# Edge counts of a graph kernel in groups of 16 destinations instead of 32

## The chip, the cores and the metric

The kernel runs on one core of one Trainium2 chip. The metric is the device time of one execution in microseconds (us); shown are the median of three runs and one profiled execution. Engines: TensorE (PE: matmuls; PEld: its weight loads), VectorE (DVE), ScalarE (ACT), GpSimd (POOL), SyncE (SP, which issues DMAs). Each engine has an instruction queue of its own, which also runs register loads, register arithmetic and branches; in the views these carry a q (DVEq). Engines meet through semaphores: an instruction counts one up when it is done, another waits until the count is high enough.

## The reference

1250 nodes with 768 features each, 40000 directed edges (src, dst) sorted by dst, and two graph blocks one after the other, each with a residual and a layer norm:

```python
def reference(x, src, dst, ...):
    # block 1: layer norm, two attention convolutions (4 heads of 192, then 2 of 96), an output product
    x = _layernorm(x + _L0_gnn_ref(x, edge_index, ...), axis=-1)
    # block 2: two normalized graph convolutions
    x = _layernorm(x + _L1_gnn_ref(x, ...), axis=-1)
    return x

def gat_conv(x, src, dst, W, a_src, a_dst, bias, H, C, n):
    h = (x @ W).reshape(n, H, C)
    e = leaky_relu(s_src[src] + s_dst[dst])
    ee = exp(e - emax[dst])                       # emax: the greatest e of each destination
    alpha = ee / denom[dst]                       # denom: their sum
    out = segment_sum(alpha[:, :, None] * h[src], dst, num_segments=n)
```

In both blocks every node also has an edge to itself. All that the edges contribute can be written with one matrix of counts, ct[source, destination] = how many edges lead from source to destination: the sums over edges become dense products with it.

## The kernel before, in words

Nodes are padded to NP = 1280 and cut into T = 10 tiles of P = 128. Edges lie in 313 chunks of 128; a unit is UC = 2 chunks, 256 edges. The kernel is written for each engine by hand; the order on each engine is the order of the code.

Setup (until about 40 us): weights are loaded and combined, the edge indices are transposed so that an edge's source and destination lie along partitions (sloT: source within its tile; keyT: source tile x 1280 + destination), and for each group of W destinations (a window; group and window mean the same below), VectorE works out which units can hold its edges, since dst is sorted. Four numbers a window go to the row rngrow: the running number of its first extra unit, the one after its last, its first unit, and the count.

Edge counts (from 41 to 204 us, the stage of the change). There are NW = 40 windows of W = 32 destinations, four (WPT) in each tile of destinations. A window takes UW = 4 fixed units from its first unit on, and then as many extra units as its edges need, in a loop whose bounds are loaded from rngrow. For each unit VectorE makes two one-hot matrices (one_hots, L512 and L513): the source one-hot ohs, 128 places x 2 chunks = 256 elements, by comparing iota with sloT, and the destination one-hot ohd, T x W = 320 columns x 2 chunks = 640 elements, which has a one in the column (source tile, destination) and is made by comparing a table vkey with key. TensorE multiplies the two for each chunk (edge_window) and sums all in one PSUM bank: 128 sources x 320 columns. Then one matmul with the identity adds the edges from a node to itself, and ScalarE copies the bank to ctmp (128 x 320). Two banks take turns.

The fixed units go through a ring of RING = 4 places; VectorE waits for a place with unit_used, TensorE for a unit with unit_ready. Extra units have two places of their own (xohs, xohd; extra_used, extra_ready). VectorE's window loads the next window's bounds from rngrow behind its first unit and its second (window_range, L306), TensorE's loads one number behind its second.

Between windows TensorE does other work of the tile: six transposes at its start, twelve dense matmuls (x times the first weights, 388 columns, three behind each window; in the last tile six behind each of the first two), and behind the first window the ten transposes of the tile before, whose counts ScalarE turns into the mask and the degrees. In the last tile VectorE makes the score vector svec before its last window, for which it waits for the last dense result. After the counts come the maxima, the attention heads, and the second block.

TensorE's matmuls of float32 are two records each in the trace.

Of the kernel before, what the change touches and what calls it, by code (L numbers as in the profile page):

```python
# [5 lines left out]
F32, BF16 = mybir.dt.float32, mybir.dt.bfloat16  # L6
# [4 lines left out]
P = 128  # L11
N, E, D = 1250, 40000, 768
T = -(-N // P)
NP = T * P
NR = N - (T - 1) * P
KD = D // P
# [6 lines left out]
W = 32  # L23
NW = NP // W
WPT = P // W
WC = T * W
# [10 lines left out]
UW = 4  # L37
# [24 lines left out]
def build(nc, t_in, out):  # L62
    ctx = ExitStack()
    with ctx:
# [34 lines left out]
        tri = at("tri", [NW, NW], F32, R_MASK + 17408)  # L99
# [31 lines left out]
        ohd_c = at("ohd_c", [P, PR, WC, 2], BF16, R_BIG + 46080)  # L131
        ohs_d = at("ohs_d", [P, PR, P, 2], BF16, R_BIG + 48640)
# [27 lines left out]
        ohs_abc = at("ohs_abc", [P, 3, PR, P, 2], BF16, R_T1)  # L160
        xohs = at("xohs", [P, 2, PR, P, 2], BF16, R_T1 + 3072)
        ohd_ab = at("ohd_ab", [P, 2, PR, WC, 2], BF16, R_T1 + 5120)
        xohd = at("xohd", [P, 2, PR, WC, 2], BF16, R_T1 + 10240)
        ohd_d = at("ohd_d", [P, PR, WC, 2], BF16, R_MASK + (T - 1) * NP * 2)
        vkey1 = at("vkey1", [P, WC, 2], I16, R_T1 + 7680)
        vkey2 = at("vkey2", [P, WC, 2], I16, R_T1 + 8960)
        vkey3 = at("vkey3", [P, WC, 2], I16, R_T1 + 1536)
# [21 lines left out]
        vkey = small("vkey", [P, WC, 2], I16)  # L189
# [120 lines left out]
        def ring_src(slot):  # L310

            return ohs_abc[:, slot, :, :, :] if slot < 3 else ohs_d[:, :, :, :]

        def ring_dst(slot):
            return ohd_ab[:, slot, :, :, :] if slot < 2 else ohd_c[:, :, :, :] if slot == 2 else ohd_d[:, :, :, :]

# [88 lines left out]
        def _(pool):  # L405
# [19 lines left out]
            step(pool.iota(vkey[:, :, :], pattern=[[NP, T], [1, W], [0, 2]], base=0, channel_multiplier=0, **io))  # L425
# [4 lines left out]
            for w, table in enumerate((vkey1, vkey2, vkey3)):  # L430
                pool.iota(table[:, :, :], pattern=[[NP, T], [1, W], [0, 2]], base=W * (w + 1), channel_multiplier=0, **io).then_inc(vkeys_set, 1)
# [11 lines left out]
        def _(v):  # L443
# [71 lines left out]
            def window(q, r, w, limits):  # L515
# [3 lines left out]
                vk, kv = (vkey, vkey1, vkey2, vkey3)[w], key[:, r, :, :]  # L519
                nxt = [end]  # L520
                for j in range(UW):
# [4 lines left out]
                    one_hots(p0, ring_src(slot), ring_dst(slot), vk, kv, unit_ready)  # L526
# [16 lines left out]
            def tile(q, r, behind, last, limits):  # L543

                v.wait_ge(v_own, V0 + q + 1)
                for w in range(3):
                    limits = window(q, r, w, limits)
# [8 lines left out]
                return window(q, r, 3, limits)  # L556
# [282 lines left out]
        def _(a):  # L839
# [54 lines left out]
            def counts_done(q, r):  # L894
                a.wait_ge(win_out, WPT * q + WPT + 2)
                copy(ct[:, :, bass.ds(q * P, P)], ctmp[:, r, :, :], ct_out)
# [10 lines left out]
            def tile(q, r, behind, last):  # L907
# [8 lines left out]
                for w in range(WPT):  # L916
                    if w == WPT - 1 and not last:
                        fixed_place(q + 1, 1 - r)
# [195 lines left out]
        def _(t):  # L1114
# [61 lines left out]
            def edge_window(q, w, limits):  # L1176
                win = WPT * q + w
                first, end = limits
                nxt = [end]
                bank = ps[:, w % 2, 0:WC]  # L1180
                t.wait_ge(win_out, win + 1)
                for j in range(UW):
                    slot = (UW * w + j) % RING
                    t.wait_ge(unit_ready, UW * win + j + 1)
                    for c in range(UC):
                        last = mm(bank, ring_src(slot)[:, c // 2, :, c % 2], ring_dst(slot)[:, c // 2, :, c % 2], j == 0 and c == 0, False, skip_group_check=True)
# [3 lines left out]
                with t.Fori(first, end) as n:  # L1190
                    place = t.snap(n % 2)
                    t.wait_ge(extra_ready, n + 1)
                    for c in range(UC):
                        last = mm(bank, xohs[:, bass.ds(place, 1), c // 2, :, c % 2], xohd[:, bass.ds(place, 1), c // 2, :, c % 2], False, c == UC - 1, skip_group_check=True)
# [369 lines left out]
```

## Time and profile before

| | us |
|---|---|
| median of three runs | 834.28 (833.35 to 835.22) |
| profiled execution | 830.65 |
| its span (first to last instruction) | 828.9 |
| granted clock of TensorE over the span | 0.977 |
| TensorE busy | 787.5 (95%) |
| VectorE busy | 588.5 (71%) |
| ScalarE busy | 296.1 (36%) |

### The profile page before, as it was taken

What the parts mean: (1) busy time and instruction counts of PE and PEld (TensorE: products, weight loads), DVE (VectorE), ACT (ScalarE), POOL (GpSimd) and SP (SyncE); (2) the same over time, 40 slices, a digit from 0 to 9 for tenths busy, and PEclk for the clock granted to TensorE, in tenths of its full rate; (3) what the DMA queues carried; (4) which work ended last, traced back from release to release, by engine and by line L of the source; (5) the groups of instructions that cost most, each with busy time, mean ns of one, the idle gap of its engine ahead of it and who ended that gap; (6) DMA issues with size and microseconds to landing.
All of it is one profiled execution on the core that took longest, in us unless ns stands there. A gap on an engine that the chain in (4) does not pass through costs nothing.

```text
span 828.9 us, 11930 instructions
## 1 busy us (share of the span) xinstructions
PE 787.5 (95%) x4286; PEld 664.6 (80%) x4286; DVE 588.5 (71%) x1210; ACT 296.1 (36%) x577; POOL 24.9 (3%) x36
## 2 busy tenths in 40 slices
PE   5899999998997999999897999899999999999997
PEld 4856666665664999999765899688898889999997
DVE  2788887885999999999698998866635532113444
ACT  4446666664532434334133454222211311111000
POOL 5100000000000400000000000000000000000000
PEclk9999999999989899999999989999999999999999
DMA  9400000000001402010000510000012000000111
GB/s 315 144 2 1 1 2 1 1 2 1 1 1 21 172 1 65 23 42 1 1 0 2 178 29 2 1 1 1 1 39 96 1 1 1 1 1 20 58 58 52
DMA packets 10540, 27.77 MB, mean 33 GB/s; under 512 B 665, under 2 KB 4075, under 8 KB 9968
## 3 DMA queue, kind: packets, MB, share of 16 engines
q1 hardware_dynamic: 10480, 26.97, 9.8%
q8 instruction: 37, 0.61, 0.3%
q14 instruction: 23, 0.19, 0.1%
HBM read 23.09 MB, written 3.88 MB: 33 GB/s over the span
## 4 chain that ended last, share of the span: by engine, by line
PE 80%; DVE 10%; issue 7%; ACT 2%; DMA 1%; SPq 1%; DVEq 0%
PE ps L1116 76%; DVE att L626 2%; DVE att L662 2%; PE ps L1205 1%; DMA edges<-in_dst 1%; PE ps L1410 1%; DVE out L649 1%; PE ps L1226 1%; PE ps L1259 1%; DVE gw1lo L706 1%; DVE scrap1b L508 0%; DVE h2x L649 0%; DVE mx L508 0%; DVE scrap L508 0%; ACT att L969 0%
## 5 line engine op out<-in xcount | busy, mean ns | idle before, releaser
L1116 PE MATMUL ps<-g,att 128*128 128x193 f32 x800 | 133.9, 331 | 6.0 <-DVE att L626 6.0
L1116 PEld LDWEIGHTS ps<-g,att 128*128 128x128 f32 x800 | 133.2, 193 | 6.8 <-issue 6.6
L969 ACT ACTIVATE att<-att,ssrc 128x1250 f32<-128x1250 f32 x60 | 80.2, 1338 | 93.2 <-DVE att L662 93.0
L626 DVE SCALAR_TENSOR_TENSOR att<-att,ct 128x1250 f32<-128x1250 f32 x60 | 88.0, 1467 | 5.0 <-ACT att L969 4.8
L662 DVE SCALAR_TENSOR_TENSOR att<-uB,s 128x1250 f32<-128x1250 f32 x60 | 91.1, 1522 | 0.0
L1116 PE MATMUL ps<-wp,xT 128*128 128x388 f32 x240 | 87.9, 504 | 0.8 <-ACT xT L913 0.8
L1116 PE MATMUL ps<-yhi,ctr 128*128 128x384 f32 x200 | 67.7, 338 | 0.0
L1116 PEld LDWEIGHTS ps<-wp,xT 128*128 128x128 f32 x240 | 42.8, 191 | 25.0 <-issue 1.3
L723 DVE SCALAR_TENSOR_TENSOR ylo_a<-ps,dinv,yhi 128x384 fp32r<-128x384 f32 x32 | 18.9, 614 | 57.5 <-ACT yhi L841 57.4
L1116 PE MATMUL ps<-h2x,att 128*128 128x97 f32 x400 | 51.0, 293 | 4.2 <-DVE att L626 2.8
L1116 PEld LDWEIGHTS ps<-h2x,att 128*128 128x128 f32 x400 | 50.3, 209 | 5.4 <-DVE att L626 4.6
L1116 PE MATMUL ps<-ylo_a,ctr 128*128 128x384 f32 x160 | 54.1, 338 | 0.0
L512 DVE TENSOR_TENSOR ohs_abc<-iota,sloT 128x256 bf16<-128x256 bf16 x120 | 34.7, 289 | 26.5 <-PE ps L1116 25.3
L841 ACT ACTIVATE yhi<-ps,dinv 128x384 fp32r<-128x384 f32 x40 | 22.0, 578 | 86.8 <-PE ps L1116 86.8
L1116 PE MATMUL ps<-ctr,yhi 128*128 128x512 f32 x180 | 44.8, 357 | 0.3 <-issue 0.3
L1116 PE MATMUL ps<-wux,xT 128*128 128x384 f32 x120 | 41.7, 504 | 0.0
L1116 PE MATMUL ps<-gw2lo,yhi 128*128 128x384 f32 x120 | 40.6, 338 | 0.0
L1116 PE MATMUL ps<-wux,xTd 128*128 128x384 f32 x120 | 40.6, 497 | 0.0
L1116 PE MATMUL ps<-gw2hi,yhi 128*128 128x384 f32 x120 | 40.4, 337 | 0.0
L513 DVE TENSOR_TENSOR ohd_ab<-vkey,key 128x640 bf16<-128x640 int16 x80 | 38.7, 483 | 0.2 <-issue 0.2
L1116 PEld LDWEIGHTS ps<-yhi,ctr 128*128 128x128 f32 x200 | 37.5, 188 | 0.0
L1116 PEld LDWEIGHTS ps<-wux,xT 128*128 128x128 f32 x120 | 23.6, 201 | 15.2 <-issue 1.7
(255 smaller groups left out, 1446.2 us busy)
## 6 DMA issues: line engine op xcount, KB each, us to landing
uB<-u_dram SPq DMA_DIRECT2D x4, 1280.0 KB, 5.9
wux<-in_L_gnn_Wu SPq DMA_DIRECT2D x2, 2304.0 KB, 15.7
gw<-in_L_gnn_W SPq DMA_DIRECT2D x2, 2304.0 KB, 10.8
xs<-in_x SPq DMA_DIRECT2D x1, 3456.0 KB
out<-ybuf SPq DMA_DIRECT2D x9, 384.0 KB, 2.3
w<-in_L_gnn_W SPq DMA_DIRECT2D x2, 1152.0 KB, 6.9
w2x<-in_L_gnn_W SPq DMA_DIRECT2D x1, 576.0 KB, 7.4
wuo<-in_L_gnn_Wu SPq DMA_DIRECT2D x1, 576.0 KB
```

The costliest lines, as they stand in the source:

```text
L512: v.tensor_tensor(src_hot, iota[:, None, :, :].to_broadcast([P, PR, P, 2]), sloT[:, bass.ds(p0, PR), None, :].to_broadcast([P, PR, P, 2]), ...
L513: v.tensor_tensor(dst_hot, vk[:, None, :, :].to_broadcast([P, PR, WC, 2]), kv[:, bass.ds(p0, PR), None, :].to_broadcast([P, PR, WC, 2]), A ...
L626: v.scalar_tensor_tensor(a, a, HUGE, ct[:, q, 0:N], ALU.min, ALU.mult).then_inc(att_ready, 1)
L649: last = v.scalar_tensor_tensor(o, src, rden[:, q:q + 1], add, ALU.mult, ALU.add)
L662: v.scalar_tensor_tensor(att[:, n % NA, 0:N], uB[:, hp % 2, 1, 0:N], s08[:, h, q:q + 1], uB[:, hp % 2, 0, 0:N], ALU.add, ALU.max).then_inc ...
L706: v.tensor_tensor(gw1lo[:, c, :], gw1[:, c, :], gw1hi(c, 0, D).bitcast(F32), ALU.subtract).then_inc(gw1_lo, 1)
L723: v.scalar_tensor_tensor(ylo(q, k * HALF, (k + 1) * HALF), ps[:, bank, 0:HALF], scale[:, q:q + 1], y(q, k * HALF, (k + 1) * HALF), ALU.mul ...
L841: a.activation(dst, src, ACT.Copy, **kw).then_inc(done, 1)
L969: a.activation(at_, at_, ACT.Exp, bias=ssrc[:, h, q:q + 1]).then_inc(att_exp, 1)
L1116: return t.matmul(o, lhsT, rhs, start=start, stop=stop, **kw)
L1205: last = t.transpose(ps[:, 4 + k, c * P - c0:(c + 1) * P - c0], ctmp[:, r, c, :], identf[:, :])
L1226: step = t.transpose(ps[:, 4 + k, c * P:(c + 1) * P], xh[:, r, kk * P:(kk + 1) * P], identf[:, :])
```

## The change

A window is now 16 destinations (W = 16): NW = 80 windows, WPT = 8 in a tile. Two windows in turn (WH = 2) fill the two halves of one PSUM bank, so that ScalarE copies as before a bank of 32 destinations, four (WPG) a tile, and the own-edge matmul is made once for both. Each window has UW = 2 fixed units; the ring still has four places. The destination one-hot of a unit has T x 16 = 160 columns, 320 elements. The eight comparison tables stand in one tensor vkeys, made by GpSimd in setup. All bounds, loads and loops that belonged to a window still do, and so there are twice as many of them.

```diff
-W = 32
+W = 16
+WH = 2
 NW = NP // W
 WPT = P // W
+WPG = WPT // WH
+WB = WH * W
...
-UW = 4
+UW = 2
...
-        vkey1 = at("vkey1", [P, WC, 2], I16, R_T1 + 7680)
...
+        ohs = at("ohs", [P, RING, PR, P, 2], BF16, R_T1)
+        ohd = at("ohd", [P, RING, PR, WC, 2], BF16, R_T1 + 3072)
+        vkeys = at("vkeys", [P, WPT, WC, 2], I16, R_T1 + 6912)
...
 # VectorE
                 for j in range(UW):
                     slot = (UW * w + j) % RING
                     v.wait_ge(unit_used, UW * win + j + 1)
                     p0 = nc.s_assert_within(v.snap((unit0 + j) * PR), 0, (UN - 1) * PR,
                                             skip_runtime_bounds_check_because="the first unit was clamped")
-                    one_hots(p0, ring_src(slot), ring_dst(slot), vk, kv, unit_ready)
+                    one_hots(p0, ohs[:, slot, :, :, :], ohd[:, slot, :, :, :], vk, kv, unit_ready)
                     if win + 1 < NW and j < 2:
                         nxt += window_range(v, win + 1, j + 1)
...
-                for w in range(3):
-                    limits = window(q, r, w, limits)
+                for w in range(WPG - 1):
+                    for half in range(WH):
+                        limits = window(q, r, WH * w + half, limits)
...
-                return window(q, r, 3, limits)
+                for half in range(WH):
+                    limits = window(q, r, WPT - WH + half, limits)
+                return limits
...
 # ScalarE
-                    a.wait_ge(win_ps, WPT * q + w + 1 + 2)
+                    a.wait_ge(win_ps, WPG * q + w + 1 + 2)
...
-                    copy(ctmp[:, r, :, w * W:(w + 1) * W], ps[:, w % 2, 0:WC].rearrange("p (a b) -> p a b", b=W), win_out)
+                    copy(ctmp[:, r, :, w * WB:(w + 1) * WB].rearrange("p a (h b) -> p a h b", b=W),
+                         ps[:, w % 2, 0:WH * WC].rearrange("p (h a b) -> p a h b", h=WH, b=W), win_out)
...
 # TensorE
-                bank = ps[:, w % 2, 0:WC]
-                t.wait_ge(win_out, win + 1)
+                bank = ps[:, group % 2, half * WC:(half + 1) * WC]
+                if half == 0:
+                    t.wait_ge(win_out, WPG * q + group + 1)
...
-                mm(ps[:, w % 2, bass.ds(q * W, W)], identb[:, :], identb[:, w * W:(w + 1) * W], False, True, skip_group_check=True).then_inc(win_ps, 1)
+                if half == WH - 1:
+                    own = ps[:, group % 2, 0:WH * WC].rearrange("p (h n) -> p h n", h=WH)[:, :, q * W:(q + 1) * W]
+                    mm(own, identb[:, :], identb[:, group * WB:(group + 1) * WB].rearrange("p (h b) -> p h b", b=W), False, True, skip_group_check=True).then_inc(win_ps, 1)
...
-                    if not last or w < 2:
-                        k = w if last else w // 2
-                        cs = range(KD) if last else range(3 * (w % 2), 3 * (w % 2) + 3)
+                    if not last or w < 2 * WH:
+                        k = w // WH if last else w // WPG
+                        cs = range(3 * (w % 2), 3 * (w % 2) + 3) if last else range((3 * (w % WPG) + 1) // 2, (3 * (w % WPG) + 4) // 2)
...
-                    if w == 0 and behind:
+                    if w == WH - 1 and behind:
```

How the change moves instructions on VectorE: a stretch of a window in the first tile before, from the load behind the second unit to the loop over the extra units (TENSOR_LOAD reads a register from rngrow; ISA and REGISTER_ALU are register arithmetic, with the wait where one is named).

```order
L306 TENSOR_LOAD rngrow
L512 ISA [waits unit_used]
L512 TENSOR_TENSOR ohs_abc<-iota,sloT 128x256
L513 REGISTER_ALU
L513 TENSOR_TENSOR ohd_c<-vkey_122,key 128x640
L512 ISA [waits unit_used]
L512 TENSOR_TENSOR ohs_d<-iota,sloT 128x256
L513 REGISTER_ALU
L513 TENSOR_TENSOR ohd_d<-vkey_122,key 128x640
L529 UNCONDITIONAL_BRANCH
L529 ISA
L512 ISA [waits extra_used]
```

And the same of the second window now, from the load behind its first unit on:

```order
L303 TENSOR_LOAD rngrow
L502 ISA [waits unit_used]
L502 TENSOR_TENSOR ohs<-iota,sloT 128x256
L503 REGISTER_ALU
L503 TENSOR_TENSOR ohd<-vkeys,key 128x320
L303 TENSOR_LOAD rngrow
L519 UNCONDITIONAL_BRANCH
L519 ISA
L502 ISA [waits extra_used]
L502 ISA
L502 TENSOR_TENSOR xohs<-iota,sloT 128x256
L503 ISA
```

Two units without a load stood between the second load and the loop; now the loop follows at once.

On TensorE, before, where the last matmuls of one window meet the next one in the first half of the second tile (identb is the own-edge matmul, wp<-xT the dense ones):

```order
L1116 MATMUL ps<-identb 128x32
L1116 MATMUL ps<-wp,xT 128x388 [waits tp_out,dn_out]
L1116 MATMUL ps<-wp,xT 128x388 x2
L1116 MATMUL ps<-ohd_ab,ohs_abc 128x320 [waits unit_ready,win_out]
L1116 MATMUL ps<-ohd_ab,ohs_abc 128x320
L1116 MATMUL ps<-ohd_ab,ohs_abc 128x320 [waits unit_ready]
L1116 MATMUL ps<-ohd_ab,ohs_abc 128x320
L306 TENSOR_LOAD rngrow
L1116 MATMUL ps<-ohd_c,ohs_abc 128x320 [waits unit_ready]
L1116 MATMUL ps<-ohd_c,ohs_abc 128x320
L1116 MATMUL ps<-ohd_d,ohs_d 128x320 [waits unit_ready]
L1116 MATMUL ps<-ohd_d,ohs_d 128x320
```

And now, behind the second window of a tile:

```order
L1110 MATMUL ps<-identb 128x2x16
L1110 MATMUL ps<-wp,xT 128x388 [waits tp_out]
L1203 MATMUL ps<-identf,ctmp 128x128 [waits win_out,tp_out]
L1203 MATMUL ps<-identf,ctmp 128x128 x9
L1110 MATMUL ps<-ohd,ohs 128x160 [waits unit_ready,win_out]
L1110 MATMUL ps<-ohd,ohs 128x160
L1110 MATMUL ps<-ohd,ohs 128x160 [waits unit_ready]
L1110 MATMUL ps<-ohd,ohs 128x160
L303 TENSOR_LOAD rngrow
L1186 UNCONDITIONAL_BRANCH
L1186 ISA
L1110 ISA [waits extra_ready]
```

The dense matmuls come in pieces of two and one, the count transposes one window later, and each window's fixed part is four matmuls of half the columns.

## Rows read from the trace of the kernel before

**Rows 1.** The page's first part: busy us (share of the span) xinstructions.

```profile
PE 787.5 (95%) x4286; PEld 664.6 (80%) x4286; DVE 588.5 (71%) x1210; ACT 296.1 (36%) x577; POOL 24.9 (3%) x36
```

**Rows 2.** Windows: stretch, length, then busy us (xinstructions) of each engine, granted clock, DMA.

```profile
core 0: us, PE busy (x) PEld busy (x) DVE busy (x) ACT busy (x) POOL busy (x), PEclk, DMA share, GB/s
41.00:203.60 162.60, 160.42 (x840) 102.48 (x840) 132.25 (x425) 97.07 (x259) 0.00 (x0) 0.99 0.01 1
58.50:185.60 127.10, 127.10 (x683) 83.33 (x682) 105.91 (x339) 82.02 (x216) 0.00 (x0) 1.00 0.00 1
41.00:58.50 17.50, 16.95 (x76) 9.30 (x77) 15.92 (x52) 6.75 (x15) 0.00 (x0) 0.90 0.01 2
```

**Rows 3.** Waits, 41 to 203.6 us: us in total, times, longest.

```profile
DVE ohs_abc L512 <- PE ps L1116: 25.3, 31, 4.3
...
DVE xohs L512 <- issue: 0.9, 2, 0.5
...
PE ps L1116 <- DVE ohd_ab L513: 0.6, 2, 0.3
```

**Rows 4.** Timeline, TensorE in a window's end: start, us, engine, line, operation.

```profile
96.91 0.73 PE L1116 MATMUL ps<-xohd,xohs 128*128 x4
...
97.48 0.18 PE L1116 MATMUL ps<-identb 128*128 128x32 bf16 x1
```

**Rows 5.** Groups of instructions by form, weight loads: busy us, mean ns.

```profile
L1116 PEld LDWEIGHTS ps<-ohd_ab,ohs_abc 128*128 128x128 bf16 x160 | 15.3, 97 | 12.7 <-issue 5.5 <-DVE ohd_ab L513 0.8
```

**Rows 6.** Timeline, VectorE in the first units of a window.

```profile
100.13 0.29 DVE L512 TENSOR_TENSOR ohs_abc<-iota,sloT 128x256 bf16<-128x256 bf16 x1 [0.36 <-PE ps L1116]
100.34 0.48 DVE L513 TENSOR_TENSOR ohd_ab<-vkey,key 128x640 bf16<-128x640 int16 x1
100.76 0.29 DVE L512 TENSOR_TENSOR ohs_abc<-iota,sloT 128x256 bf16<-128x256 bf16 x1
...
101.39 0.29 DVE L512 TENSOR_TENSOR ohs_abc<-iota,sloT 128x256 bf16<-128x256 bf16 x1
...
102.00 0.28 DVE L512 TENSOR_TENSOR ohs_d<-iota,sloT 128x256 bf16<-128x256 bf16 x1
```

**Rows 7.** Line 306, register loads: count, ns min/median/max, first and last start us.

```profile
L306 DVEq TENSOR_LOAD <-rngrow x81: 298/301/559, 39.8 to 195.2; - x81
```

**Rows 8.** VectorE around a loop of two turns: line 529, 92.3 to 96.6, and timeline.

```profile
L529 DVEq COMPARE_BRANCH  x2: 43/62/80, 94.8 to 95.8; - x2
L529 DVEq MOVE  x1: 36/36/36, 93.9 to 93.9; - x1
...
93.75 0.29 DVE L512 TENSOR_TENSOR ohs_d<-iota,sloT 128x256 bf16<-128x256 bf16 x1
...
94.48 0.29 DVE L512 TENSOR_TENSOR xohs<-iota,sloT 128x256 bf16 x1
...
95.51 0.29 DVE L512 TENSOR_TENSOR xohs<-iota,sloT 128x256 bf16 x1 [0.34 <-issue]
```

**Rows 9.** Line 529, VectorE's loop over extra units, all of the stage.

```profile
L529 DVEq FUSED_REGOPS  x46: 51/51/51, 43.0 to 201.5; - x46
L529 DVEq ALU_OP  x46: 40/40/47, 43.7 to 202.2; - x46
L529 DVEq COMPARE_BRANCH  x46: 43/43/80, 43.8 to 202.3; - x46
```

**Rows 10.** Timeline, start of a tile: TensorE's transposes, ScalarE's scaling, the dense matmuls.

```profile
106.50 0.82 PE L1226 MATMUL ps<-identf,xh 128*128 128x128 f32 x6
...
107.19 2.22 ACT L913 ACTIVATE xT<-ps,gcol 128x128 f32<-128x128 f32 x6
...
108.60 2.20 PE L1116 MATMUL ps<-wp,xT 128*128 128x388 f32 x6
```

**Rows 11.** Timeline, the stage's first one-hot, the last tile's dense matmuls, the stage's end.

```profile
41.28 0.29 DVE L512 TENSOR_TENSOR ohs_abc<-iota,sloT 128x256 bf16<-128x256 bf16 x1 [0.89 <-DVE key L540]
...
195.23 4.16 PE L1116 MATMUL ps<-wp,xT 128*128 128x388 f32 x12
...
204.21 0.18 PE L1116 MATMUL ps<-identb 128*128 128x32 bf16 x1
```

More of the change, by code:

```diff
@@ L424, in _ @@
             step(pool.memset(farc[:, :], FAR))
-            step(pool.iota(vkey[:, :, :], pattern=[[NP, T], [1, W], [0, 2]], base=0, channel_multiplier=0, **io))
+            step(pool.iota(vkeys[:, 0, :, :], pattern=[[NP, T], [1, W], [0, 2]], base=0, channel_multiplier=0, **io))
             step(pool.iota(iota[:, :, :], pattern=[[1, P], [0, 2]], base=0, channel_multiplier=0, **io))
@@ L429, in _ @@
             pool.wait_ge(const_a, 1)
-            for w, table in enumerate((vkey1, vkey2, vkey3)):
-                pool.iota(table[:, :, :], pattern=[[NP, T], [1, W], [0, 2]], base=W * (w + 1), channel_multiplier=0, **io).then_inc(vkeys_set, 1)
+            for w in range(1, WPT):
+                pool.iota(vkeys[:, w, :, :], pattern=[[NP, T], [1, W], [0, 2]], base=W * w, channel_multiplier=0, **io).then_inc(vkeys_set, 1)
             for wu, loaded in ((wux, wux_in), (wux2, wux2_in)):
@@ L518, in window @@
                 first, end, unit0 = limits
-                vk, kv = (vkey, vkey1, vkey2, vkey3)[w], key[:, r, :, :]
+                vk, kv = vkeys[:, w, :, :], key[:, r, :, :]
                 nxt = [end]
@@ L915, in tile @@
                     step.then_inc(tp_out, 1)
-                for w in range(WPT):
-                    if w == WPT - 1 and not last:
+                for w in range(WPG):
+                    if w == WPG - 1 and not last:
                         fixed_place(q + 1, 1 - r)
@@ L1177, in edge_window @@
                 win = WPT * q + w
+                group, half = w // WH, w % WH
                 first, end = limits
                 nxt = [end]
-                bank = ps[:, w % 2, 0:WC]
-                t.wait_ge(win_out, win + 1)
+                bank = ps[:, group % 2, half * WC:(half + 1) * WC]
+                if half == 0:
+                    t.wait_ge(win_out, WPG * q + group + 1)
                 for j in range(UW):
@@ L1185, in edge_window @@
                     for c in range(UC):
-                        last = mm(bank, ring_src(slot)[:, c // 2, :, c % 2], ring_dst(slot)[:, c // 2, :, c % 2], j == 0 and c == 0, False, skip_group_check=True)
+                        last = mm(bank, ohs[:, slot, c // 2, :, c % 2], ohd[:, slot, c // 2, :, c % 2], half == 0 and j == 0 and c == 0, False, skip_group_check=True)
                     last.then_inc(unit_used, 1)
@@ L1193, in edge_window @@
                     for c in range(UC):
-                        last = mm(bank, xohs[:, bass.ds(place, 1), c // 2, :, c % 2], xohd[:, bass.ds(place, 1), c // 2, :, c % 2], False, c == UC - 1, skip_group_check=True)
+                        last = mm(bank, xohs[:, bass.ds(place, 1), c // 2, :, c % 2], xohd[:, bass.ds(place, 1), c // 2, :, c % 2], False, False, skip_group_check=True)
                     last.then_inc(extra_used, 1)
-                mm(ps[:, w % 2, bass.ds(q * W, W)], identb[:, :], identb[:, w * W:(w + 1) * W], False, True, skip_group_check=True).then_inc(win_ps, 1)
+                if half == WH - 1:
+                    own = ps[:, group % 2, 0:WH * WC].rearrange("p (h n) -> p h n", h=WH)[:, :, q * W:(q + 1) * W]
+                    mm(own, identb[:, :], identb[:, group * WB:(group + 1) * WB].rearrange("p (h b) -> p h b", b=W), False, True, skip_group_check=True).then_inc(win_ps, 1)
                 return nxt
             def count_transposes(q, r):
-                t.wait_ge(win_out, WPT * q + WPT + 2)
+                t.wait_ge(win_out, WPG * q + WPG + 2)
                 for k, (c0, c1) in enumerate(PIECES):
@@ L1229, in tile @@
                     limits = edge_window(q, w, limits)
-                    if w == 2 and last:
+                    if w == 3 * WH - 1 and last:
                         t.wait_ge(vec_ready, 1)
```

20 lines of the change are left out of this document (4 added, 16 removed).

## The prediction

> **What bounds the kernel now.** I read the page first: TensorE is busy for 95% of the span and VectorE for 71% [rows 1]. The change touches one stage only, the edge counts, so I then read the stage by windows of time. From 41.0 to 203.6 us TensorE is busy 160.4 of 162.6 us at a granted clock of 0.99; in the eight full tiles between 58.5 and 185.6 us it is busy all the time at 1.00, 15.9 us a tile, while VectorE is busy 105.9 of 127.1 [rows 2]. The view of waits says the same: VectorE waits 25.3 us for TensorE before its one-hots, in 31 places, and TensorE waits for VectorE 0.6 us in all [rows 3]. So TensorE sets this stage and VectorE is the follower, with 21 us to spare by its busy time.
>
> **TensorE's side.** One unit (256 edges) is two matmuls. Four matmuls of the extra units start at 96.91 and the next instruction at 97.48, so one of 320 columns takes (97.48 - 96.91)/4 = 0.141 us [rows 4]. How many there are follows from the destinations, which are sorted: counting the aligned units that each group touches gives 46 extra units with groups of 32 (the trace has the 46 loop turns [rows 9] and 92 matmuls), and 87 with groups of 16, since 73 of the 80 groups touch three units and 7 touch four. Matmuls go from (160 + 46) x 2 = 412 to (160 + 87) x 2 = 494, each with 160 columns. No row has such a matmul. From below the price is the columns alone, half of 0.141, about 0.075; from above it is 0.141, if the weight load of 0.097 [rows 5] or the issue held the pace. I take 0.085, near the lower end, because the same weight load is hidden now. TensorE then spends 494 x 0.085 = 42.0 instead of 412 x 0.141 = 58.1 us, 16 less over ten tiles.
>
> The Trainium skill ("TensorE: Matmul & The Clock Gate", Back-to-back issue gap) says that the pace of such a stream is set by weight load and matmul together, 81 ns at 128 columns and 131 at 512. An estimate between these gives 85 ns at 160 columns, but the same line would give 106 at 320, where the trace has 141; so the page is not followed as a scale.
>
> Something is given back at each tile's start. The transposes start at 106.50, ScalarE begins to scale them at 107.19 and has six done after 2.22, so the first three at 108.3; TensorE came to its dense matmuls at 108.60 [rows 10]. Behind one small group it comes there at about 107.15 + 0.5 = 107.7 and waits 0.6, nine or ten times. All other moved pieces (twelve dense matmuls a tile in pieces of two and one instead of three, the count transposes behind the second group, the own-edge matmul for two groups at once) are the same work in the same order, and ScalarE has the same four copies a tile; it is busy 97 of 162.6 us [rows 2], which hides a slower copy.
>
> **VectorE's engine side.** A unit is two comparisons. From start to start the source one-hot (256 elements) takes 0.21 and the destination one-hot (640) 0.42 [rows 6]. With 320 elements it lies between these; on the line through both 0.24. A unit falls from 0.61 to 0.45 and a group of three units takes 1.35 on the engine. That is far below TensorE's pace, so by busy time nothing is lost.
>
> **VectorE's queue side.** Per group its queue does two register loads, one for each of the first two units, and one loop for the extra units. It did this once for 32 destinations and now does it once for 16.
> - A register load takes 0.301 [rows 7]. The two units with a load start 0.63 apart (100.13, 100.76, 101.39), the next one without a load 0.61 [rows 6]. So with a load the queue needs 0.63 and the engine no longer sets the step. Shorter comparisons don't shorten it. In the new group both fixed units carry a load: 1.26.
> - The loop: its first register move is at 93.9, its first branch at 94.8, the second turn's branch at 95.8 [rows 8]. One turn is 0.9 to the branch and 0.1 on to the next wait: 1.0, say 0.95. The engine shows it too: the second extra unit starts 1.03 after the first, with 0.34 idle put down to issue [rows 8]. So a second turn costs 1.03.
> - Together 2.2 us a group (1.26 + 0.95). Before, with two units more, it was 2.2 + 2 x 0.3 = 2.8 against an engine time of 3.05 and TensorE's 3.5 to 4, so it showed nowhere. Now it stands against 1.35 of the engine and, from TensorE's side, (15.9 - 1.6)/8 = 1.8 of a group's mean. The queue is the longest of the three.
>
> From below, if all register work ran beside the comparisons, a group would be 1.35 and TensorE's 1.8 would count; from above, 2 x 0.63 + 1.03 = 2.3. I take 2.2: the pieces come from stretches in which the engine had run empty.
>
> The Trainium skill ("DMA: Bandwidth & Descriptors", Latency and other measured facts) puts a floor of about 600 ns on a register load; the 81 loads of VectorE here take 301 [rows 7]. By the page a group would be 2.8 and the stage 48 us longer still; the trace decides.
>
> **The sum.** The first one-hot starts at 41.28 [rows 11]. 80 groups x 2.2 = 176.0; 7 second turns x 1.03 = 7.2; each tile's key and extra wait about 0.15, 1.5 in all (an estimate from register operations of 0.04 to 0.05 [rows 9]). This gives 226.0.
> - Ordinary tiles don't add to it. At a tile's start TensorE needs about 0.9 for transposes, 0.5 and 1.4 for the first group and its dense matmuls, 0.5, 0.7 and 1.3 for the second with the count transposes, 5.3 to 5.9 against VectorE's 4.4; VectorE may be two groups ahead (four ring places, two units a group), so it isn't stopped.
> - The last tile does. There TensorE does twelve dense records (4.15 us, six matmuls) per 32 destinations in its first half [rows 11]; with transposes and count transposes the first four groups take it about 13 us against VectorE's 8.8, and VectorE may be two groups ahead. Written out step by step, its fifth group waits 1.3 for the third's ring places, its sixth 0.5, and the score vector 1.5 for the last dense result: 3.3 (none at least, 5 at most).
> - Behind VectorE's last branch TensorE ends 0.9 later (its wait, two matmuls, own edges).
> So the last own-edge matmul comes at 226.0 + 3.3 + 0.9 = 230.2, where it is now at 204.2 [rows 11]: +26.0. What follows is the same work and moves with it. The profiled execution has a span of 828.9 and took 830.65; it becomes 856.7. The median of the three runs shown is 834.28, 3.6 above the profiled one, so I forecast 860 us. With 2.1 to 2.3 a group and the last tile at 0 to 5 the likeliest case's own range is 852 to 868.
>
> **Rivals.**
> - *TensorE stays the bound and gets shorter.* If VectorE's queue runs its loads and the loop beside the comparisons, a tile is 15.9 - 1.6 + 0.6 = 14.9 us, ten tiles give -10: 824 us (819 with matmuls at 0.075 and 830 at 0.097). For it: VectorE hardly ever idled by issue before, 0.9 us at one-hots of extra units [rows 3]. Against it: that was with 2.8 of queue work below 3.05 of engine work, and the 1.03 step. It decides below a queue time of 1.85 us a group.
> - *The weight load or the issue holds TensorE's matmuls at 0.141.* Then 494 x 0.141 = 69.7, +11.6, with the tile starts +17: 851 us, if the queue of VectorE is below that (17.6 a tile are 2.2 a group, so the two would be even). Against it: the weight load's 0.097 is below 0.141.
> - *Part of the queue work is hidden.* With 2.0 us a group, for example if the loop's first turn overlaps the last fixed unit: 16 less, 844 us. For it: before, a loop's first turn followed the last fixed unit after 0.73 (93.75 to 94.48 [rows 8]), though this is from comparison to comparison and not to the next group.
> - *A group's pace is right but the clock falls,* since TensorE now idles 15 to 20% of the stage. In the first tile, where it started from idle, the granted clock was 0.90 [rows 2]. Its matmuls have room below VectorE's pace; even at half the clock in a tenth of the stage this is below 2 us and lies in the range.
>
> **How the numbers follow.** Queue of VectorE at 2.1 to 2.3: 0.82 (860). TensorE bound and shorter: 0.07 (824). TensorE at 0.141: 0.05 (851). Partly hidden: 0.06 (844). A difference under 0.2% is about what a measurement of this kernel can't tell from none. Faster has the 824 case, 0.06; within 0.2% 0.02, where it would meet the other losses by chance; slower 0.92. The range 848 to 868 leaves out the 824 and 844 cases and little at the top.
>
> **What the new profile would show.** Right: VectorE's one-hots with idle before them put down to issue, not to TensorE; TensorE's edge matmuls waiting for VectorE's one-hots, some 30 to 40 us idle in the stage (26 and what its matmuls get shorter); fixed units 0.63 apart, groups 2.2, tiles 18.5; 160 register loads on VectorE; the stage's end near 230. Destination one-hots near 0.24 from start to start and edge matmuls near 0.085 would confirm the terms that don't count. Wrong: TensorE busy all through the stage; fixed units 0.45 apart; or a loop's turn that costs nothing because its operations run under the comparisons.

## The result, and the profile after

| | before | after |
|---|---|---|
| median, measured side by side (us) | 834.66 | 858.4 (856.92 to 861.11) |
| ratio, 95% interval | | 1.029 (1.027 to 1.032) |
| span of the profiled execution | 828.9 | 855.2 |
| its granted clock | 0.977 | 0.970 |

The changed kernel is 2.9% slower. The forecast was 860. The page's first part, to be read against [rows 1]:

```profile
PE 788.8 (92%) x4368; PEld 665.2 (78%) x4368; DVE 584.2 (68%) x1292; ACT 297.0 (35%) x577; POOL 25.3 (3%) x40
```

The busy times differ by 4 us at most, VectorE's is even shorter, and the span is 26.3 us longer: the time went into idleness. The windows of time show where (the first is the stage, as [rows 2]; the third is what follows it):

```profile
41.00:228.20 187.20, 160.39 (x924) 101.32 (x924) 127.60 (x507) 97.54 (x259) 0.00 (x0) 0.97 0.01 2
41.00:60.50 19.50, 16.60 (x78) 9.61 (x79) 13.61 (x54) 5.05 (x13) 0.00 (x0) 0.79 0.01 2
228.20:252.80 24.60, 23.32 (x96) 17.84 (x96) 21.31 (x37) 12.26 (x28) 0.00 (x0) 0.76 0.00 1
```

The same stretch after the stage in the kernel before:

```profile
204.20:228.80 24.60, 23.07 (x105) 16.59 (x105) 21.77 (x37) 12.44 (x29) 0.00 (x0) 0.93 0.00 1
```

Of the 26.3 us, 24.0 are the stage (its last own-edge matmul moves from 204.21 to 228.22) and 2.3 come behind it, where the granted clock is 0.76 instead of 0.93. The waits inside the stage, beside [rows 3] (us in total, times, longest):

```profile
DVE xohs L502 <- issue: 40.3, 74, 0.9
PE ps L1110 <- DVE xohd L503: 13.3, 23, 1.0
PE ps L1110 <- ACT xT L906: 10.8, 9, 1.5
DVE xohs L502 <- PE ps L1110: 7.2, 12, 0.9
```

Before, VectorE waited 25.3 us for TensorE and 0.9 for issue. Now TensorE waits for VectorE, and VectorE, before 74 of its extra units, waits for nothing that another engine does. "issue" is its own queue. The timeline of VectorE shows one such group after the other, beside [rows 6, 8]:

```profile
107.45 0.29 DVE L502 TENSOR_TENSOR ohs<-iota,sloT 128x256 bf16<-128x256 bf16 x1
107.66 0.32 DVE L503 TENSOR_TENSOR ohd<-vkeys,key 128x320 bf16<-128x320 int16 x1
108.08 0.29 DVE L502 TENSOR_TENSOR ohs<-iota,sloT 128x256 bf16<-128x256 bf16 x1
108.29 0.32 DVE L503 TENSOR_TENSOR ohd<-vkeys,key 128x320 bf16<-128x320 int16 x1
109.15 0.29 DVE L502 TENSOR_TENSOR xohs<-iota,sloT 128x256 bf16 x1 [0.55 <-issue]
109.36 0.32 DVE L503 TENSOR_TENSOR xohd<-vkeys,key 128x320 int16 x1
109.62 0.29 DVE L502 TENSOR_TENSOR ohs<-iota,sloT 128x256 bf16<-128x256 bf16 x1
```

Read the source one-hots from start to start: 0.63 with a load behind the first unit, 1.07 with a load and the loop's first turn, 0.47 to the next group: 2.17 us. Another extra unit idles 0.54 "for PE" (at 105.97). Of the 12 idle times that make up the 7.2 us above, nine are 0.52 to 0.55 long, as those put down to issue. An idle time of the same length at the same place is most likely the same cause, so most of the 7.2 us belong to the queue too.

### The profile page after: what moved, and what is told of

Read it like the earlier page. It is cut to its first block, busy times and chain, and to the rows that moved or that the text cites. A ratio compares the mean times of both kernels' runs of the same rounds, so it can differ in the third digit from the quotient of the medians.

```text
span 855.2 us, 12872 instructions
## 1 busy us (share of the span) xinstructions
PE 788.8 (92%) x4368; PEld 665.2 (78%) x4368; DVE 584.2 (68%) x1292; ACT 297.0 (35%) x577; POOL 25.3 (3%) x40
## 4 chain that ended last, share of the span: by engine, by line
PE 70%; DVE 12%; issue 9%; ACT 4%; DVEq 4%; DMA 1%; SPq 1%
PE ps L1110 67%; DVE att L619 2%; DVE att L655 2%; DVEq L303 2%; DVEq L502 2%; PE ps L1203 1%; ACT xT L906 1%; ACT ct L834 1%; PE ps L1408 1%; DMA edges<-in_dst 1%; DVE xohd L503 1%; DVE ohs L502 1%; ACT g L896 1%; DVE ohd L503 1%; DVE gw1lo L699 1%
## 5 line engine op out<-in xcount | busy, mean ns | idle before, releaser
L1110 PE MATMUL ps<-wp,xT 128*128 128x388 f32 x240 | 99.6, 528 | 11.8 <-ACT xT L906 10.8
L1110 PEld LDWEIGHTS ps<-wp,xT 128*128 128x128 f32 x240 | 40.6, 195 | 28.0 <-issue 14.6
L502 DVE TENSOR_TENSOR xohs<-iota,sloT 128x256 bf16 x87 | 25.4, 292 | 47.7 <-issue 40.3
L502 DVE TENSOR_TENSOR ohs<-iota,sloT 128x256 bf16<-128x256 bf16 x160 | 46.6, 291 | 10.5 <-issue 1.7
L503 DVE TENSOR_TENSOR ohd<-vkeys,key 128x320 bf16<-128x320 int16 x160 | 50.9, 318 | 0.2 <-issue 0.2
L1110 PEld LDWEIGHTS ps<-ohd,ohs 128*128 128x128 bf16 x320 | 27.4, 99 | 24.6 <-issue 14.4
L834 ACT ACTIVATE ctmp<-ps 128x320 f32<-128x320 f32 x40 | 17.5, 438 | 77.7 <-PE ps L1110 77.6
L1110 PE MATMUL ps<-xohd,xohs 128*128 x174 | 30.8, 239 | 13.6 <-DVE xohd L503 13.3
```

What stands on the lines that cost most here:

```text
L502: v.tensor_tensor(src_hot, iota[:, None, :, :].to_broadcast([P, PR, P, 2]), sloT[:, bass.ds(p0, PR), None, :].to_broadcast([P, PR, P, 2]), ...
L503: v.tensor_tensor(dst_hot, vk[:, None, :, :].to_broadcast([P, PR, WC, 2]), kv[:, bass.ds(p0, PR), None, :].to_broadcast([P, PR, WC, 2]), A ...
L834: a.activation(dst, src, ACT.Copy, **kw).then_inc(done, 1)
L1110: return t.matmul(o, lhsT, rhs, start=start, stop=stop, **kw)
```

## The experiments

All kernels made for them keep the bounds of the groups as 16-bit instead of 32-bit numbers. Each was timed beside the kernel before, runs 1 to 8 on one chip and runs 9 to 11 on another, where the kernel before took the same time (medians 834.41 and 833.85, and 834.53). "Stage" is from VectorE's first one-hot to the last own-edge matmul, from each run's timeline.

| kernel | median | ratio (interval) | stage |
|---|---|---|---|
| before | 833.85 to 834.66 | 1 | 41.28 to 204.21 |
| after | 858.4 | 1.029 (1.027 to 1.032) | 41.30 to 228.22 |
| 1 control | 859.05 | 1.028 (1.023 to 1.032) | 44.03 to 228.22 |
| 2 one packed load | 856.99 | 1.028 (1.022 to 1.034) | 40.70 to 226.80 |
| 3 third load | 883.04 | 1.058 (1.055 to 1.061) | 42.95 to 250.66 |
| 4 half one-hot | 857.84 | 1.027 (1.024 to 1.031) | 41.59 to 225.63 |
| 5 before, more loads | 853.78 | 1.024 (1.020 to 1.028) | 42.54 to 223.60 |
| 6 no loop | 829.54 | 0.995 (0.993 to 0.998) | 40.59 to 198.99 |
| 7 loop skipped | 834.28 | 0.999 (0.997 to 1.001) | 43.48 to 204.29 |
| 8 early transposes | 818.24 | 0.980 (0.976 to 0.985) | 40.68 to 187.26 |
| 9 before, early transposes | 834.91 | 1.001 (0.999 to 1.002) | 43.17 to 206.26 |
| 10 after, early transposes | 854.35 | 1.023 (1.020 to 1.026) | 42.77 to 226.17 |
| 11 as 8, two loads | 824.79 | 0.989 (0.986 to 0.991) | 42.79 to 193.96 |

The stage's start differs by up to 3.4 us between profiles, and setup isn't what the experiments change (but for how the bounds are packed); so a difference of medians below some 3 us is not explained here. What is compared below is the pace of groups and the length of the stage.

**1. Control.** The changed kernel with the 16-bit row.

```diff
-        rngrow = small("rngrow", [1, NW * 4], I32)
+        rngrow = small("rngrow", [1, NW * 4], U16)
```

> The changed kernel with the row of bounds held as 16-bit instead of 32-bit integers, nothing else; the next kernels are built on it. Both theories (VectorE's instruction queue sets the stage; TensorE's matmuls or its weight loads set it) expect the changed kernel's time, 858 us, with register loads of 0.30 us as before. If a 16-bit load costs another price, the time moves by 80 x 2 x the difference.

859.05: as expected. A 16-bit load takes 285 ns (median of 161) instead of 301, a group with one extra unit 2.14 us instead of 2.17 (medians of 72), and the stage 184.2 instead of 186.9; the median time doesn't show it. The experiments on the changed kernel are read against the control.

**2. One packed load a group.** The first unit and the number of extra units come in one number, and the queue takes them apart.

```diff
+            p = nc.values_load(rngrow[0:1, bass.ds(4 * w + 1, 1)], ...)
+            return eng.snap(p & 255), eng.snap(p >> 8)
...
-                first, end, unit0 = limits
+                first, unit0, count = limits
+                end = v.snap(first + count)
...
-                    if win + 1 < NW and j < 2:
-                        nxt += window_range(v, win + 1, j + 1)
+                    if win + 1 < NW and j == 1:
+                        nxt += packed(v, win + 1)
```

> Each window's first unit and count of extra units stand in one number, so VectorE's queue loads once instead of twice a window and gains two or three register operations; the work of both engines is the same. Queue theory: a window falls from 2.17 by 0.35 and gains about 0.15, 80 windows: 858 - 16 = 842 us (838 to 848). Theory that the engines' own work or TensorE's weight loads set the stage: 858, no change.

856.99: a miss by 15 us. The timeline shows what happened to the saved load:

```profile
101.55 0.29 DVE L508 TENSOR_TENSOR ohs<-iota,sloT 128x256 bf16<-128x256 bf16 x1 [0.52 <-issue]
...
101.99 0.28 DVE L508 TENSOR_TENSOR ohs<-iota,sloT 128x256 bf16<-128x256 bf16 x1
...
103.02 0.29 DVE L508 TENSOR_TENSOR xohs<-iota,sloT 128x256 bf16 x1 [0.51 <-issue]
...
103.70 0.29 DVE L508 TENSOR_TENSOR ohs<-iota,sloT 128x256 bf16<-128x256 bf16 x1 [0.15 <-issue]
```

The step without a load fell from 0.63 to 0.44, but the way from the extra unit to the next group rose from 0.47 to 0.68: the sum and the unpacking that the packed number needs are queue work as well. This group takes 2.15, and the median one 2.13 where the control has 2.14. The rival's number (858, no change) is the one that came out. But the experiment didn't lower the queue's total, so it doesn't tell the theories apart; that is left to runs 3 and 4. It shows only that here a register load was traded for register arithmetic at no gain.

**3. A third load a group.** The opposite direction: only more queue work.

```diff
+                    if win + 1 < NW and j == 1:
+                        nxt += window_range(v, win + 1, 2)
```

> The changed kernel (with the 16-bit row of bounds, as the control, 859.05) in which VectorE's queue loads a third number for each window: the window's first unit once more, for the extra loop's use. 242 register loads instead of 162, no other work on any engine. Theory (VectorE's queue sets the pace of a window): every window gets 0.30 to 0.35 us longer, the step that a load takes in the control's trace; 80 x 0.30 to 0.35 = 24 to 28 us, so 883 to 887 us. Rival (VectorE's engine or TensorE sets the pace, and the queue runs ahead of them): nothing changes, 857 to 861 us.

883.04, 24.0 over the control. The timeline of a group:

```profile
108.30 0.29 DVE L502 TENSOR_TENSOR ohs<-iota,sloT 128x256 bf16<-128x256 bf16 x1
...
108.91 0.29 DVE L502 TENSOR_TENSOR ohs<-iota,sloT 128x256 bf16<-128x256 bf16 x1
...
110.30 0.29 DVE L502 TENSOR_TENSOR xohs<-iota,sloT 128x256 bf16 x1 [0.86 <-issue]
...
110.77 0.29 DVE L502 TENSOR_TENSOR ohs<-iota,sloT 128x256 bf16<-128x256 bf16 x1
```

The idle time before the extra unit is 0.86 where the control has 0.53, and the median group takes 2.46 instead of 2.14. The stage is 207.7 us long instead of 184.2: 23.5 us for 80 loads, 0.29 each. In these groups the load shows in full; in the last tile some of it is taken back, because VectorE no longer waits there for TensorE (1.39 + 0.23 us in the control). Nothing was added to TensorE, to its queue or to VectorE's engine, so none of them sets this pace.

**4. Half of the destination one-hot.** Less engine work, the same queue work. The other half of the columns stays zero, so the counts of half of the source tiles are left out.

```diff
-                v.tensor_tensor(dst_hot, vk[:, None, :, :]..., ALU.is_equal).then_inc(done, 1)
+                v.tensor_tensor(dst_hot[:, :, 0:HCUT, :], vk[:, None, 0:HCUT, :]..., ALU.is_equal).then_inc(done, 1)
```

> The changed kernel (16-bit row) whose destination one-hots compare only the first half of the columns; the other half is zero from the start, so that half of the source tiles' counts is left out. All matmuls, loads, loops and waits stay. VectorE's engine gets 247 x about 0.09 = 22 us less to do. Theory (the queue sets the pace): nothing changes, 857 to 861 us. Rival (the engine's comparisons set it): 837 to 842 us.

857.84: no change. A destination one-hot takes 0.23 us instead of 0.32, and the idle time takes the difference over (0.62 where the control has 0.53). A group is 2.15 (106.41 to 108.56), and the stage has the control's length within 0.2 us:

```profile
106.41 0.29 DVE L503 TENSOR_TENSOR ohs<-iota,sloT 128x256 bf16<-128x256 bf16 x1
...
108.09 0.29 DVE L503 TENSOR_TENSOR xohs<-iota,sloT 128x256 bf16 x1 [0.62 <-issue]
...
108.56 0.29 DVE L503 TENSOR_TENSOR ohs<-iota,sloT 128x256 bf16<-128x256 bf16 x1
...
109.17 0.29 DVE L503 TENSOR_TENSOR ohs<-iota,sloT 128x256 bf16<-128x256 bf16 x1 [0.17 <-issue]
109.38 0.23 DVE L504 TENSOR_TENSOR ohd<-vkeys,key 128x160 bf16<-128x160 int16 x1
```

Runs 3 and 4 together show that VectorE's queue, and not its engine, sets the changed kernel's pace.

**5. The kernel before with four more loads a group.** Is it the queue as such, or something in the groups of 16?

```diff
+                    elif win + 1 < NW:
+                        nxt += window_range(v, win + 1, 2, 2)
```

> The kernel before (groups of 32, 16-bit row) with four more register loads a window on VectorE, five in six of its loads without other use: 242 loads instead of 82. Theory: VectorE's queue then needs 2.8 + 4 x 0.30 to 0.35 = 4.0 to 4.2 us for a group of 32, where TensorE needs 15.9/4 = 3.97 on average; the time rises only by what stands over TensorE's pace, 40 x 0.0 to 0.25 plus the tiles in which TensorE is quicker: 837 to 846 us, and VectorE's idle time goes from TensorE to issue. Rival (loads run beside the comparisons and the queue never counts): 834 to 836 us, with VectorE waiting for TensorE as before.

853.78: the direction is the theory's, the size 8 us over its range. The waits of the stage, beside [rows 3]:

```profile
DVE xohs L512 <- issue: 29.2, 45, 1.1
...
DVE ohs_abc L512 <- PE ps L1118: 8.8, 11, 3.1
```

The queue takes over from TensorE in the old groups as well. A group without a second turn starts at 106.68 and the next at 110.91, the one after it at 115.10:

```profile
106.68 0.28 DVE L512 TENSOR_TENSOR ohs_abc<-iota,sloT 128x256 bf16<-128x256 bf16 x1
...
110.91 0.28 DVE L512 TENSOR_TENSOR ohs_abc<-iota,sloT 128x256 bf16<-128x256 bf16 x1
...
115.10 0.28 DVE L512 TENSOR_TENSOR ohs_abc<-iota,sloT 128x256 bf16<-128x256 bf16 x1
```

That is 4.2, the upper end expected. What I had left out: the six second turns (6 x 1.0), and the 8.8 us that VectorE still waits for TensorE, 3.1 of it in one place of the last tile. I had compared two means and taken the larger; but where TensorE is slow for a while the queue waits, and where TensorE is quick the queue can't catch up. 40 x 4.2 + 6.0 + 8.8 = 182.8, where the profile has 181.1.

**6. Three fixed units and no loop.** The fourth unit of the seven groups that need one is left out.

```diff
-UW = 2
+UW = 3
...
-                with v.Fori(first, end) as n:
-                    ...
```

> Three fixed units a window and no loop on either engine, two register loads a window kept; the fourth unit of seven windows is left out. 240 units instead of 247, so the engines' work is almost the same. Queue theory: the loop's 0.95 us a window becomes 0.3 for a third fixed unit, the queue needs 1.55, TensorE is the bound again and its edge matmuls at 0.073 show: a tile of about 14.3 us instead of 15.9 before, 834.7 - 16 = 819 us (814 to 826). Theory that TensorE's matmuls (0.141 each, or the weight load) set the stage: 850 or more.

829.54, 3.5 us over the expected range: the 30 us come back, and then ten more were expected. The waits show why they don't come:

```profile
DVE ohs L502 <- PE ps L1103: 34.2, 45, 2.7
...
PE ps L1103 <- ACT xT L899: 14.9, 9, 1.7
```

VectorE waits for TensorE again, and TensorE waits nine times 1.7 us for ScalarE's scaled transposes at a tile's start. In the changed kernel this wait (10.8) was beside the queue's; now it is on the path.

**7. The whole computation with the loop skipped.** Three fixed units, a ring of six places, the packed load, and the loop inside a branch that 73 of the 80 groups don't enter.

```diff
+                with v.If(count > 0):
+                    first = earlier(v, win)
+                    with v.Fori(first, first + count) as n:
```

> The whole computation: three fixed units a window, a ring of six places, one register load for first unit and count, and the loop over further units behind a branch that 73 of 80 windows jump over; inside it one more load. Queue theory: a window of about 0.63 + 0.3 + 0.3 + 0.2 for the branch = 1.45, below TensorE's 1.8: 821 us (815 to 830), faster than both kernels. If a branch that is taken costs more than 0.5 us, the queue stays the bound: 835 or more. Theory that TensorE's matmuls set the stage: 850 or more.

834.28, where the kernel before lies, and a miss: 821 was expected. The number alone would also suit the case of a dear branch (835 or more), in which the queue stays the bound. But where VectorE isn't held up a group takes 1.47 us (it starts at 44.96, 46.43 and 47.90), so the branch is not dear; and TensorE waits for xT as in run 6, 14.4 us in nine places. Runs 6 and 7 left one question: are the waits for xT all that keeps this form from a gain?

**8. The transposes early.** As run 7; TensorE issues the next tile's transposes before the last two groups of a tile, and ScalarE scales them before it copies the last bank. For this ScalarE also makes the next tile's rows, which the transposes read, one bank earlier (not in the cut below).

```diff
+                    if w == WPT - 2 and not last:
+                        transposed(q + 1, 1 - r)
...
+                    if w == WPG - 1 and not last:
+                        scaled(q + 1, 1 - r)
```

> The whole computation. As the run with three fixed units, one load and a skipped loop (834.28), and besides the next tile's six transposes are issued on TensorE before the window before last, and ScalarE scales them (xT) before it copies the last group of the tile, so that a tile's first dense matmul finds xT ready. Theory: in that run TensorE waited 9 times 1.6 to 1.7 us for xT, and VectorE behind it; without these waits 834.3 - 15 = about 820 us (815 to 828), below both kernels, with no wait for xT left. Rival: ScalarE, busy some 12 to 13 us a tile, sets the pace once the group copies come behind the scaling, and TensorE waits for win_out instead: 830 us or more.

818.24 (814.25 to 820.43), 2.0% below the kernel before. No wait for xT is left among the stage's waits; the largest of VectorE's are:

```profile
DVE ohs L513 <- PE ps L1130: 10.8, 24, 2.2
...
DVE xohs L513 <- issue: 6.9, 10, 1.1
```

TensorE is busy again nearly all the time:

```profile
41.00:186.50 145.50, 140.90 (x927) 97.01 (x924) 120.68 (x511) 97.13 (x259) 0.00 (x0) 1.00 0.01 2
```

And VectorE, where it isn't held up, gives a group every 1.48 us (0.44, 0.44 and 0.60 with the load):

```profile
96.97 0.29 DVE L513 TENSOR_TENSOR ohs<-iota,sloT 128x256 bf16<-128x256 bf16 x1 [0.16 <-issue]
...
97.41 0.28 DVE L513 TENSOR_TENSOR ohs<-iota,sloT 128x256 bf16<-128x256 bf16 x1
...
97.85 0.28 DVE L513 TENSOR_TENSOR ohs<-iota,sloT 128x256 bf16<-128x256 bf16 x1
...
98.45 0.29 DVE L513 TENSOR_TENSOR ohs<-iota,sloT 128x256 bf16<-128x256 bf16 x1
```

**9 and 10. The early transposes alone**, in the kernel before and in the changed kernel, with the edit of run 8.

> The kernel before (groups of 32, 16-bit row) with the same move of the transposes and the scaling. Theory: TensorE is busy all through the stage there and comes to its first dense matmul of a tile after xT is ready, so there is no wait to take away: 833 to 836 us. Rival (the gain of the run at 818.24 comes from the moved transposes and not from the groups of 16): about 818 us.

> The changed kernel (16-bit row, control 859.05) with only the transposes and ScalarE's scaling of a tile moved ahead into the tile before; groups, units, loads and loops as they are. Theory (VectorE's queue sets the pace at 2.17 us a group, and TensorE's waits of 1.4 us for xT lie beside it): about the same, 856 to 860 us, with less TensorE waiting for xT and more waiting for VectorE. Rival (the nine waits for xT are part of the loss): 9 x 1.4 = 13 us less, 844 to 848 us.

834.91 and 854.35. In the kernel before the move is worth nothing, since TensorE doesn't wait for xT there. In the changed kernel it takes 4.7 us off the control's median, not the 13 of nine waits; the theory had at most 3. By the timelines the stage is only 0.8 us shorter than the control's (183.4 and 184.2), and this is the last tile, where VectorE waits 0.45 us for TensorE instead of 1.39. The profiled spans differ by 4.4 us: the stage starts 1.3 earlier, is 0.8 shorter, and what follows it takes 2.4 less, where the second ten matmuls take 1.34 us instead of 2.40. Why these were quicker is open. So neither the groups of 16 nor the early transposes give the gain of run 8; they give it together, once the queue is out of the way.

**11. Run 8 with two loads again.**

```diff
-                nxt += packed(v, win + 1)
+                nxt += window_range(v, win + 1, j + 1)      # for j = 0 and j = 1
...
-                with v.If(count > 0):
+                with v.If(end > first):
```

> The whole computation. As the run at 818.24 (three fixed units, loop skipped where it has no turn, transposes early), but with two register loads a group again in place of one packed number: 162 loads instead of 80 on VectorE. Theory (queue work is free as long as it and the engine stay under TensorE's pace): in that run VectorE gives a group every 1.48 us where it isn't held up (0.44, 0.44 and 0.60 between units), the second load makes one of the 0.44 into 0.63 and drops two register operations, 1.6 to 1.7, and TensorE's mean is (187.3 - 41.3)/80 = 1.82: within 5 us of it, 816 to 824 us. Rival (each load costs its 0.30 to 0.35 wherever it stands): 80 x 0.3 = 24 less what the dropped operations give back (80 x 0.2), at least 8 us, or up to 842 us.

824.79, just over the theory's range, 6.6 over run 8 by the medians and 4.6 by the length of the stage. A group is 1.62 instead of 1.48 (106.98 less 105.36), as expected:

```profile
105.36 0.29 DVE L502 TENSOR_TENSOR ohs<-iota,sloT 128x256 bf16<-128x256 bf16 x1
...
106.98 0.29 DVE L502 TENSOR_TENSOR ohs<-iota,sloT 128x256 bf16<-128x256 bf16 x1
```

That is below TensorE's mean of 1.83 in run 8 (146.6/80) but not below its pace between the transposes. There a group is six matmuls of 0.0725 and on average three dense records of 0.345 (four in 103.09 - 101.71, in the rows of the next section), 1.47 us: run 8's queue is level with it at 1.48, and this one is 0.14 over it. An estimate from this: some 60 groups lie between the transposes, so at most 60 x 0.14 = 8 us; measured are 4.6. A likely reason, not shown, is that VectorE catches up while TensorE does its transposes. Again a mean hid it, as in run 5.

## Why the prediction was right, step by step

- *The bound moves to VectorE's queue.* Right, and shown by runs 3 and 4, with run 5 as the counterpart in the old groups. The rival "TensorE stays the bound" (824) needed less than 1.85 us of queue work a group; it had 2.17. It would have become true only with the loop skipped (runs 6 to 8).
- *2.2 us a group.* Measured 2.17. The pieces were 0.63, right, and (0.63 + 0.95) = 1.58 for the rest, measured 1.07 + 0.47 = 1.54. The rival "partly hidden" (2.0) is out.
- *Second turns at 1.03.* Measured 1.01 (105.97 to 106.98). There are 87 extra units in 80 loops, as counted.
- *TensorE's matmul of 160 columns.* Four in (103.38 - 103.09), 0.0725 each; I took 0.085 and had half of 0.141 as the lower bound. (The subtraction in the prediction gives 0.1425; over eight such matmuls, 95.78 to 96.91, it is 0.141. The sum doesn't hang on it.) The price is nearly in proportion to the columns:

```profile
101.71 1.54 PE L1110 MATMUL ps<-wp,xT 128*128 128x388 f32 x4 [1.44 <-ACT xT L906]
103.09 0.45 PE L1110 MATMUL ps<-ohd,ohs 128*128 128x160 bf16 x4
103.38 0.30 PE L1110 MATMUL ps<-xohd,xohs 128*128 x2
```

- *The wait at a tile's start.* Predicted 0.6, measured 1.44 here and 10.8 in nine places. I had let ScalarE start its scaling 0.7 after the first transpose, as before [rows 10]. Now it starts 1.58 after it (98.82 to 100.40), because TensorE reaches the transposes while ScalarE still has the tile before to close, its copy of the counts and the dense results. Behind a tile's last own-edge matmul TensorE has two dense records now and had six, so the transposes come 0.76 us behind that matmul (98.06 to 98.82) instead of 2.07 (104.43 to 106.50):

```profile
98.75 1.27 ACT L834 ACTIVATE ct<-ctmp 128x1280 uint16<-128x1280 f32 x1
98.82 0.82 PE L1224 MATMUL ps<-identf,xh 128*128 128x128 f32 x6
...
99.92 0.47 ACT L896 ACTIVATE g<-ps 128x384 f32<-128x384 f32 x1
...
100.40 2.22 ACT L906 ACTIVATE xT<-ps,gcol 128x128 f32<-128x128 f32 x6
```

The wait didn't count, since it lay beside the queue's, but it is the term that decided runs 6 and 7. A step that costs nothing under today's bound should still be sized.
- *The last tile.* Predicted 3.3, measured 1.31 + 0.20 + 0.66 = 2.2:

```profile
217.71 0.29 DVE L502 TENSOR_TENSOR ohs<-iota,sloT 128x256 bf16<-128x256 bf16 x1 [1.31 <-PE ps L1110]
...
220.14 0.29 DVE L502 TENSOR_TENSOR ohs<-iota,sloT 128x256 bf16<-128x256 bf16 x1 [0.20 <-PE ps L1110]
...
223.03 0.18 DVE L544 CAST svec<-ssrc 128x40 fp32r<-128x40 f32 x1 [0.66 <-ACT sdst L834]
```

- *The stage's end.* Predicted 230.2, measured 228.22: 80 x 0.03 = 2.4 less for the groups and 1.1 less for the last tile, which leaves 1.5 more. The timeline shows where they are. Eleven groups take 2.48 to 2.66, some 4 us in all (last section), and the groups at 64.10 and 67.62, where the granted clock was 0.87 and VectorE waited for TensorE, are 0.5 too long together; against this stand seventeen groups of 2.10 to 2.13. The mean of a group, with all this in it, is 2.21. So 2.2 was right as a mean partly by luck: it has no pauses in it.
- *TensorE idle for 30 to 40 us in the stage.* By busy time it is 187.2 - 160.4 = 26.8. In its first 19.5 us the granted clock was 0.79 (0.90 before, [rows 2]), and a matmul at a lower clock is busy longer (see the ten matmuls below); the shorter matmuls don't show in full.
- *What follows the stage moves with it.* Wrong by 2.3 us. I looked for the price of a lower clock inside the stage; it came behind it. In the stage's last 6 us TensorE was busy for 3.64 us (4.96 before). From 228.2 to 237.2 the granted clock was 0.50, the lower of the two levels, and the ten matmuls that come next took 2.37 us instead of 1.31; before, it was 1.00 up to the stage's end, 0.87 from 204.2 to 207.2 and 0.56 from 207.2 to 210.2:

```profile
228.22 0.20 PE L1110 MATMUL ps<-identb 128*128 128x32 bf16 x1
228.26 2.37 PE L1110 MATMUL ps<-sRow,sel 104*128 104x128 f32 x10
```

The two errors, -2.0 in the stage and +2.3 behind it, cancel: the profiled execution was forecast at 856.7 and took 856.92, which is luck. The 1.6 us by which the forecast of 860 misses the median come from a third term: 3.6 were added for the distance from the profiled execution to the median, and this time it was 1.5.

- *The Trainium skill.* Its floor of about 600 ns on a register load ("DMA: Bandwidth & Descriptors", Latency and other measured facts) didn't hold here. The 161 loads have a median of 301 ns:

```profile
L303 DVEq TENSOR_LOAD <-rngrow x161: 298/301/559, 39.8 to 224.2; - x161
```

Run 3 says the same by the length of the stage: each further load costs 0.29 us. The line through the Trainium skill's 81 and 131 ns ("TensorE: Matmul & The Clock Gate", Back-to-back issue gap) gave 85 ns at 160 columns, an estimate; the trace has 72.5 there and 141 at 320, nearly in proportion to the columns.

## What to carry to other kernels

An engine's busy share says nothing about its queue: before a loop body is made smaller, count the register loads, loops and branches that stay per body, take their price from a place where the engine idles "for issue", and compare it with the new body. Smaller pieces paid here (2.0%) only when the loop was skipped wherever it had no turn and the next waiting thing, the transposes at a tile's start, was moved ahead. Compare such paces piece by piece and not by their means: twice here a queue below or near the other engine's mean cost 5 to 8 us more than the means had said (runs 5 and 11).

## What the runs showed of the hardware

- Register arithmetic in VectorE's queue is not cheap beside a load: taking one load away and adding the unpacking and one sum left the median group at 2.13 instead of 2.14 us (run 2 beside the control).
- The granted clock fell behind a stretch in which TensorE idled, and what came next paid the price. With groups of 32 (before, runs 5 and 9) TensorE was busy for 4.9 to 5.0 of the stage's last 6 us, the clock stayed at 1.00 to the stage's end, and the ten matmuls behind it took 1.31 us. In all kernels with groups of 16 it was busy for 3.4 to 3.9 us, and for 4.6 in run 6; the clock fell in or just behind the last 3 us, and the ten matmuls took 2.37 or 2.38 us, 2.24 in run 6. So it is in runs 8 and 11 too, which are faster than the kernel before. In run 5 the second ten matmuls took 2.06 us (1.33 before).
- In some groups the idle time for issue is longer by a third of a microsecond, for example 1.23 instead of 0.86 in run 3, at 107.82. In the changed kernel eleven groups are longer by this, one in every six or seven. The profile names no cause, and it stays open:

```profile
107.82 0.29 DVE L502 TENSOR_TENSOR xohs<-iota,sloT 128x256 bf16 x1 [1.23 <-issue]
```
